# First sequence of a macaron block: weight rounding in pieces, FIR weights on GpSimd, small loads on a second queue

## What is computed

```python
def block(x):
    x = x + 0.5 * ffn(layernorm(x))
    x = x + attn(layernorm(x))
    return x + 0.5 * ffn(layernorm(x))

def ffn(x):                       # 256 -> 1024 -> 256, the same weights both times
    return gelu(x @ w1 + b1) @ w2 + b2

def attn(x):
    q, k, v = (silu(causal_conv4(x @ W)) for W in (Wq, Wk, Wv))   # 4 heads of 64
    delta = delta_rule(l2norm(q), l2norm(k), v, sigmoid(x @ Wb))  # chunks of 32
    branches = [fir(v, fir_s), fir(v, fir_l), delta, v]           # 3 and 31 taps
    w = gate(x, branches)                                         # softmax of an MLP on x and the branches
    o = sum(w[i] * branches[i])
    return rmsnorm(o) * onorm_w @ Wo
```

## Time and profile before

| what | us |
|---|---|
| median of 3 runs (lowest, highest) | 1275.45 (1259.55, 1276.28) |
| the profiled execution's own time | 1264.83 |
| its span, first to last instruction | 1263.1 |
| busy in the span: PE, DVE, ACT, POOL | 1084.4, 827.3, 545.9, 408.9 |
| mean granted TensorE clock | 0.926 of full |

### The profile page before, as it was taken

One profiled execution on the slowest core, in us unless ns is written; L12 is line 12 of the kernel. 1 busy time (PEld: TensorE's weight loads), 2 busy tenths in 40 slices (PEclk: granted clock), 3 DMA queues, 4 the chain that ended last, 5 costly groups with the idle time before them and its releaser, 6 DMA issues.

```text
span 1263.1 us, 25583 instructions
## 1 busy us (share of the span) xinstructions
PE 1084.4 (86%) x10348; PEld 807.0 (64%) x10348; DVE 827.3 (65%) x1548; ACT 545.9 (43%) x957; POOL 408.9 (32%) x640
## 2 busy tenths in 40 slices
PE   3768597799988998899979996899988998888728
PEld 2654485388745885488737884388736885477327
DVE  5773357685687667875787666775787667763263
ACT  1153136443374337543564335453464337432312
POOL 8007400661018500771048200851038300850000
PEclk9888699899999999999999998899999999895758
DMA  5040104110040204010140204010040204020000
GB/s 149 1 108 10 32 1 94 24 31 19 18 101 1 50 13 97 10 30 20 35 85 1 49 18 95 6 33 19 18 101 1 50 1 97 5 50 1 1 0 17
DMA packets 80245, 47.19 MB, mean 37 GB/s; under 512 B 55808, under 2 KB 73728, under 8 KB 80128
## 3 DMA queue, kind: packets, MB, share of 16 engines
q1 hardware_dynamic: 80128, 45.56, 16.0%
HBM read 30.86 MB, written 14.68 MB: 36 GB/s over the span
## 4 chain that ended last, share of the span: by engine, by line
PE 59%; DVE 22%; ACT 6%; issue 5%; SPq 3%; POOL 3%; DMA 2%; DVEq 0%; POOLq 0%; ACTq 0%
PE psum L767 12%; PE psum L769 10%; PE psum L768 10%; DVE conv_acc L1333 5%; PE psum L798 4%; DVE arena L1564 3%; PE psum L953 3%; PE psum L938 2%; PE psum L972 2%; PE psum L977 2%; SPq L346 2%; PE psum L1130 2%; DVE arena L1566 2%; PE psum L893 1%; PE psum L908 1%
## 5 line engine op out<-in xcount | busy, mean ns | idle before, releaser
L515 POOL TENSOR_TENSOR l_prod<-arena 64x30 f32<-64x30 f32 (+14 forms) x240 | 148.6, 619 | 616.4 <-DMA arena<-l_dram 598.2
L566 ACT ACTIVATE h_f<-psum,b_col 128x512 f32<-128x512 f32 x128 | 88.0, 688 | 227.2 <-PE psum L769 210.3
L519 POOL TENSOR_TENSOR arena<-arena,l_prod 64x30 f32<-64x30 f32 (+14 forms) x240 | 158.5, 660 | 18.8
L767 PE MATMUL psum<-w_hi,h_hi 128*128 128x256 f32 x512 | 152.2, 297 | 9.6 <-DVE h_lo L1313 9.5
L769 PE MATMUL psum<-w_hi,h_lo 128*128 128x256 f32 x512 | 145.1, 283 | 0.0
L768 PE MATMUL psum<-w_lo,h_hi 128*128 128x256 f32 x512 | 145.1, 283 | 0.0
L1059 PE MATMUL psum<-v_shift,fir_w 128*32 128x512 f32 x1152 | 139.1, 620 | 5.1 <-DMA v_shift<-v_dram 5.1
L1333 DVE SCALAR_TENSOR_TENSOR conv_acc<-psum,conv_col,conv_acc 128x511 f32<-128x511 f32 x144 | 107.8, 748 | 34.3 <-ACT conv_acc L591 22.9
L1312 DVE CAST h_hi<-h_f 128x512 fp32r<-128x512 f32 x128 | 78.9, 617 | 71.0 <-ACT h_f L566 39.2
L767 PE MATMUL psum<-xt_hi,w_hi 128*128 128x512 f32 x256 | 109.8, 429 | 15.9 <-DVE b_half L1426 7.0
L798 PE MATMUL psum<-ident,arena 128*128 128x128 f32 x384 | 56.4, 301 | 67.5 <-DVE arena L1576 45.2
(11 more groups left out here) (224 smaller groups left out, 2243.6 us busy)
## 6 DMA issues: line engine op xcount, KB each, us to landing
x_in<-in_L_attn_x SPq DMA_DIRECT2D x8, 512.0 KB, 3.8
v_dram<-v_fm SPq DMA_DIRECT2D x8, 512.0 KB, 2.8
v_shift<-v_dram SPq DMA_DIRECT2D x8, 512.0 KB, 5.1
out<-x_tok SPq DMA_DIRECT2D x8, 512.0 KB, 2.9
v_shift<-v_dram SPq DMA_DIRECT2D x8, 511.0 KB, 7.2
v_shift<-v_dram SPq DMA_DIRECT2D x8, 510.0 KB, 9.3
v_shift<-v_dram SPq DMA_DIRECT2D x8, 509.0 KB, 11.8
arena<-in_L_ffn_w SPq DMA_DIRECT2D x2, 1024.0 KB, 7.2
```

What stands on the lines that cost most here:

```text
L515: pool.tensor_tensor(prod, l_inv[:, k + 1:, k:k + 1].broadcast_to(shape), l_inv[:, k:k + 1, 0:k].broadcast_to(shape), ALU.mult).then_inc(i ...
L519: pool.tensor_tensor(l_inv[:, k + 1:, 0:k], l_inv[:, k + 1:, 0:k], prod, ALU.add).then_inc(inverted, 1)
L566: act.activation(h_f[:, m % 2, :], bank, ACT.Gelu, bias=b1_col[:, m:m + 1]).then_inc(read, 1)
L767: pe.matmul(dst, a_hi, b_hi, start=first, stop=False, **kw)
```

## The change

- Small loads: SyncE keeps the first 20 of the 57 (the biases, the taps, the weights of convolution and gate). The other 37 (`temp_col`, `gb2_col`, `floor_b`, `onorm_col`, `wb_pad`, `w2g_pad`) are issued by ScalarE, at the start of its program, behind the same five memsets. The semaphore and its count stay.
- wqkv is split in three pieces of 512 columns behind the splits of h 0, 1 and 2 instead of at once behind h 0; wh comes behind h 3 instead of h 1.
- `fir_weights` leaves VectorE and becomes GpSimd's, behind the adds of `b2_half` to x_in, with a wait for `c_loaded` ahead and a wait for its own semaphore, `fir_w_made`, behind each instruction. TensorE waits for `fir_w_made` ahead of its first FIR matmul.
- VectorE's wait for the constants and the small loads moves from behind h 3 to behind h 7.
- TensorE begins the feed-forward when w1 is split (`SETUP_W1` = 2) and waits for the rest of `SETUP_FFN` ahead of down 0.

```diff
-        CONST_MADE, C_LOADED, SETUP_DVE = 60, 57, 36
+        CONST_MADE, C_LOADED, SETUP_DVE = 60, 57, 32
         ZEROED, IDENT_MADE = 5, 7
-        SETUP_FFN, SETUP_LARGE = 5, 26
+        SETUP_W1 = 2
+        SETUP_FFN, SETUP_LARGE = 5, 22
...
-            for h in range(HEADS):
-                load(temp_col[32 * h:32 * h + 32, :], temp[h:h + 1].partition_broadcast(32))
...
-            assert loads == C_LOADED, ("C_LOADED", loads)
...
+            def fir_weights(s):
+
+                rows = slice(32 * s, 32 * s + 32)
+                shape = [32, GROUPS, TAPG, 32]
+                e = eye32[rows, :].unsqueeze(1).broadcast_to([32, GROUPS * TAPG, 32]).rearrange("p (g n) c -> p g n c", g=GROUPS)
+                tap = taps_l[rows, :, 3 - s:3 - s + 4 * (TAPG - 1) + 1:4]
+                pool.tensor_tensor(fir_w[rows, :, 0:TAPG, :], e, tap.unsqueeze(3).broadcast_to(shape), ALU.mult) \
+                    .then_inc(fir_w_made, 1)
+                pool.wait_ge(fir_w_made, 2 * s + 1)
+                pool.tensor_tensor(fir_w[rows, :, TAPG, :], eye32[rows, :].unsqueeze(1).broadcast_to([32, GROUPS, 32]),
+                                   taps_s[rows, :, 3 - s:4 - s].broadcast_to([32, GROUPS, 32]), ALU.mult).then_inc(fir_w_made, 1)
+                pool.wait_ge(fir_w_made, 2 * s + 2)
...
                     last.then_inc(bias1_added, 1)
                     pool.wait_ge(bias1_added, j + 1)
+                    if not at.back:
+                        pool.wait_ge(c_loaded, C_LOADED * 16)
+                        for s in range(CONV):
+                            fir_weights(s)
...
         def _(act):
+            def load(dst, src, **kw):
+                act.dma_start(dst, src, **kw).then_inc(c_loaded, 16)
+
+            act.wait_ge(const_made, ZEROED)
+            for h in range(HEADS):
+                load(temp_col[32 * h:32 * h + 32, :], temp[h:h + 1].partition_broadcast(32))
+                swap = (1, 0) if h % 2 else (0, 1)
+                for slot, b in enumerate(swap):
+                    load(gb2_col[32 * h + slot:32 * h + slot + 1, :], gb2[b:b + 1].rearrange("(p a) -> p a", a=1))
+                    load(floor_b[:, h, slot:slot + 1], eps_floor[h, b:b + 1].partition_broadcast(P),
+                         allow_slow_non_contiguous=True)
+                load(gb2_col[32 * h + 2:32 * h + 4, :], gb2[2:4].rearrange("(p a) -> p a", a=1))
+                load(floor_b[:, h, 2:4], eps_floor[h, 2:4].partition_broadcast(P))
+            for h in range(2):
+                load(onorm_col[D * h:D * h + D, :], onorm_w.rearrange("(p a) -> p a", a=1))
+            load(wb_pad[:, :, 0:HEADS], Wb.rearrange("(k p) n -> p k n", p=P))
+            for par in range(2):
+                load(w2g_pad[:, par, 2:4], gW2[:, 2:4])
+                for slot, b in enumerate((1, 0) if par else (0, 1)):
+                    load(w2g_pad[:, par, slot:slot + 1], gW2[:, b:b + 1], allow_slow_non_contiguous=True)
             act.wait_ge(ffn_loaded, 4 * 16)
...
-                    pe.wait_ge(setup_dve, SETUP_FFN)
+                    pe.wait_ge(setup_dve, SETUP_W1)
                     for n in range(len(STEPS)):
+                        if STEPS[n] == ("down", 0, 0):
+                            pe.wait_ge(setup_dve, SETUP_FFN)
                         ffn_step(at, 0, j, n)
...
                 if at.front:
+                    if not at.back:
+                        pe.wait_ge(fir_w_made, 2 * CONV)
                     pe.wait_ge(v_shifted, 64 * j + 64)
                     firs(at, 0, range(0, 1))
...
                         if m == 0:
                             dve.wait_ge(w_loaded, 5 * 16)
-                            split_weights(wqkv_hi, wqkv_lo, wqkv_st)
-                        elif m == 1:
+                        if m < 3:
+                            split_weights(wqkv_hi[:, KQV[m]], wqkv_lo[:, KQV[m]], wqkv_st[:, KQV[m]])
+                        elif m == 3:
                             split_weights(wh_hi, wh_lo, wh_st)
-                        elif m == 3:
+                        elif m == 7:
                             dve.wait_ge(const_made, CONST_MADE)
                             dve.wait_ge(c_loaded, C_LOADED * 16)
-                        if 3 <= m < 7:
-                            fir_weights(m - 3)
-                        elif m == 7:
                             small_weights()
```

More of the change, by code:

```diff
@@ L290, in macaron_kernel @@
         t_stored, t_loaded = sem("t_stored"), sem("t_loaded")
+        fir_w_made = sem("fir_w_made")
         fir_done = sem("fir_done")
@@ L340, in _ @@
             sp.sem_inc(y_stored, 1)
-            loads = 0
             def load(dst, src, **kw):
-                nonlocal loads
-                loads += 1
                 sp.dma_start(dst, src, **kw).then_inc(c_loaded, 16)
@@ L1216, in split_weights @@
                 step(dve.tensor_tensor(lo[dims], staged, hi[dims].bitcast(F32), ALU.subtract))
[L1218 to L1226, removed]
             def small_weights():
```

## The result

| | before | after |
|---|---|---|
| median of 18 runs each, us | 1272.49 | 1284.7 |
| lowest to highest | 1259.55 to 1283.8 | 1272.57 to 1292.9 |
| profiled execution, its span | 1264.83, 1263.1 | 1284.07, 1282.4 |

The ratio is 1.0092, with a 95% interval of [1.0068, 1.0116]: 12 us slower, between 9 and 15. Within 2%, and clear of noise.

What follows compares the result with a forecast made beforehand. TensorE carries 59% of the chain, VectorE 22%; in the first sequence every delay delays the span. 1264.8 - 3.9 + 6.7 - 12.8 + 1.0 + 22.2 = 1278.0 us, own range 1273 to 1284 (chance 0.62), wide range 1254 to 1294.

Steps and rivals of the forecast that it cites:

- the landmark: End of the second `x_tok` residual in the first sequence, 61.85 us before the change, forecast near 75.0.
- rival B: ScalarE's loads at 0.60 us each, with GpSimd shutting VectorE out: 6.7 us more, 1284.7; chance 0.08.
- start without w2's rounding: TensorE's feed-forward start: waiting for w1 alone, no longer behind 4.05 us of w2 rounding, saves 3.9 us.
- ScalarE's 37 loads: Start of ScalarE: loads take 15.5 us as on SyncE, delaying the square root and so TensorE by 6.7 us.
- long and short multiply: FIR weights on GpSimd: a 32x2048 multiply takes 4.3 us, a 32x256 one 0.7, 20 us for all eight.
- restart of TensorE behind split 3: Feed-forward after the fourth split of h (counted from 0): TensorE restarts at its lower clock, costing 2.3 us.
- shutting out in all: First feed-forward: GpSimd's multiplies keep VectorE out of its splits, ending the residuals 22.2 us later than 52.8.
- The loads: Small loads, issued from SyncE and ScalarE: all complete by about 27.5 us, the last having landed at 42.66 before.
- The rule on the port: SBUF: two-SBUF-input or fast-copy VectorE instructions and SBUF-reading GpSimd instructions block each other throughout; used for the +22.2 us.
- A: Feed-forward: the multiplies don't shut VectorE out for their whole length, or are much faster; 1255.8 us, chance 0.16.
- C: Feed-forward: half the shutting out, 10 us instead of 22.2, giving 1265.8 us; chance 0.09.
- D: Small loads share the same DMA engines and still land at 42.7; +6, 1270.8 us, chance 0.05.

Runs made afterwards that it cites:

- FIR weights last: Changed kernel with small loads back on SyncE and GpSimd's FIR weights behind VectorE's gate weights: ratio to before 0.9856; with loads left on ScalarE, 1.0006.

## Why the prediction was right, and where its steps were not

The forecast was +13 us and the landmark at 75.0; measured were +12 [+9, +15] and 77.06. The mechanism was the one named: VectorE shut out one instruction at a time, by multiplies that fall on the feed-forward, and a late square root. But two terms were off by 10 and 8.5 us, in opposite ways, and that the total came out is luck in good part.

The time itself, 1284.7, lies just above my own range of 1273 to 1284. I had added the +13.2 to the profiled execution, 1264.8; added to the median of 18 runs, 1272.49, it gives 1285.7. That 1284.7 is also the number of rival B is chance: B's difference was +20. But B's sign, a start of TensorE beyond 30, came true, and mine (the square root near 18.9, TensorE near 25.7) did not.

| step | predicted | measured |
|---|---|---|
| start without w2's rounding | -3.9 | -3.8: at 35.85, where `b_half` was made at 39.56 |
| ScalarE's 37 loads | 15.5 us, +6.7 | 25.5 us, +16.75 |
| feed-forward from start to residual, not held up | 27.1 | 27.5 (FIR weights last) |
| long and short multiply | 4.3 and 0.7 | 3.75 and 0.62 alone, 3.80 and 0.96 beside VectorE |
| from the first multiply to the end of the eighth | 24.0 | 19.6 |
| restart of TensorE behind split 3 | at the lower clock, +2.3 | at full clock |
| shutting out in all | +22.2 | +13.7 |

- **ScalarE's loads.** The mis-sized term is "if they take as long here". I took the duration from a stretch in which SyncE was the only queue and the big weights had landed, and moved it to where neither holds. Alone, ScalarE takes the 15.5 us. My rival B (0.60 each, 22.2 us) was nearer; even it was short by 3 us. The mechanism of the delay, all of it reaching TensorE, was right.
- **The multiplies.** The slope of the short products (3.9) was better than the one with the adds in it (4.4). And a turn of VectorE costs GpSimd less than its listed duration: a pair of multiplies repeats every 4.92 us (43.79 to 48.71), and every 4.53 with nothing beside it that it shuts out (57.48 to 62.01, FIR weights last): 0.39 us more, where I had added 1.12 for a cast and a subtraction.
- **TensorE's clock.** Behind the idle of 5.44 us down 2 and the up step ran at the lower level (granted clock 0.52 from 58.0 to 63.4), but their time lay under the multiplies. Split 3 follows split 2 by 6.4 us only, so TensorE then idled 1.03, and from 64.4 on the granted clock was 1.00: its matmul at 64.46 is listed with 0.38, against 0.58 at 58.04. I had taken the long idle for all three.
- **The 8.5 us of the shutting out.** Of these, 4.4 are the multiplies, 2.1 the clock, and 1.4 that the multiplies began 7.9 us behind TensorE's start instead of 9.3. The rest of 0.6 is spread over small differences.
- **The loads.** Expected complete by 27.5. SyncE's own queue ends at 28.90 + 3.81 = 32.71, since its issues were stretched too. It was hidden: GpSimd came to them at 43.79.
- **The rule on the port** (the Trainium skill, "SBUF — State Buffer", section "Who interferes with whom"): the traces agree at 3.8 us too. By the same section an instruction of VectorE with at most one input in SBUF, and outside the fast modes, is not held up; they agree here as well: a convolution step, one input in PSUM and one in SBUF, runs beside a multiply at its own 0.77 us.
- **The rule on issuing engines** (the Trainium skill, "DMA: Bandwidth & Descriptors", section "Issuing engines are not separate DMA queues") grants that a second engine saves issue time. I trusted the saving because issue time was the large part. The runs show less: the 57 small loads were all issued at 32.71 instead of 37.65. That is 5 us saved for a ScalarE that is busy for 25.

Rivals: A (gain kept) is out by the 4.12 us rows. C is out as a mechanism, since the whole multiply blocks, but its 10 us are nearer to the 13.7 than my 22.2. B is dealt with above. D is out: nothing waited for a small load.

What stays open: the head pass is 15.7 us longer to the merge and the kernel 12 [9, 15]; with the FIR weights last it is 13.4 shorter there and the kernel 18 [12, 24]. The profiles say how much of such a difference need not come from the head. From the merge to the end, where the change touches nothing, they take 1115.6 us (before), 1119.2 (after), 1123.3 (FIR weights last) and, in the others, up to 1130.4. That scatter is as large as the differences to be explained; whether any of it hangs on how the head pass ends was not tried.

## What to carry to other kernels

Look at what VectorE does beside a place before giving work to GpSimd there. Here the convolutions, which read PSUM and one SBUF tile, and a reduce of one SBUF tile ran beside the multiplies unhindered; casts, subtractions and small tensor_scalars from SBUF to SBUF waited. Price a place by the length of GpSimd's single instructions, not by its idle time. Loads issued by an engine that computes stand in front of its first instruction; when that is the head of the chain, moving issue time there can cost more than it frees (here 16.75 us on the square root for 5 us of issuing). A part that loses beside another can win alone, as the FIR weights on GpSimd did with the loads back on SyncE: try the parts of a change one by one. And remove the wait that ends last first: the early start was worth nothing until the FIR weights and their wait for the loads had left the splits.

## What the runs showed of the hardware that I had not expected

- Two queues that issue at once stretch each other: 37 small loads take 15.5 us from either engine alone, 25.5 us from ScalarE beside SyncE's big and small ones; single issues of 0.35 us grow to 2.22. What they share was not found out.
- Between back-to-back instructions of GpSimd VectorE gets its turn without any wait in GpSimd's program (a subtraction of 4.11 beside a multiply of 3.80), which the cast of 3.94 us at 273.71 had seemed to exclude. That cast stays unexplained.
- Even a tensor_scalar of 32x128 from SBUF to SBUF, 0.25 us alone, waits out a multiply: eight took 9.15 us. A tensor_reduce of 128x1024 from SBUF does not (1.22 us either way).
